# A graph network kernel: GpSimd's streams of gathers and scatters are paused in five different ways

## The reference, cut to what matters

```python
h = relu(layernorm(x)); x = x + gat(gat(h))          # attention over edges, 3 heads x 32, then 1 x 32
h = relu(layernorm(x)); x = x + rgcn(relu(rgcn(h)))  # per relation r: mean over its edges of h[src] @ W[r]
h = relu(layernorm(x)); x = x + f(h) + segment_sum(w * h[src] * h[dst] / (...), src)
h = relu(layernorm(x)); x = x + segment_sum((h[src] @ W_rel[type]) * e, dst)
```

## Time and profile before

| | us |
|---|---|
| median of 2 runs | 8182.64 (8157.38 to 8207.9) |
| the profiled execution | 8155.02 |
| its span | 8153.3 |
| GpSimd busy | 4271.4 (52%), 3949 instructions |
| VectorE busy | 3662.5 (45%) |
| TensorE busy with matmuls | 3196.6 (39%) |
| pass k, its 56 gathers | starts 1632.9 to 1705.5 |
| pass g1, its 336 gathers | starts 1752.0 to 2197.5 |
| pass g2, its 392 gathers | starts 2657.1 to 3258.0 |
| pass r1, its 392 gathers | starts 3537.0 to 4057.9 |
| pass r2, its 392 gathers | starts 4562.7 to 5158.4 |
| pass l2, its first gather | starts 5452.3 |
| pass l3, its gathers, then its scatters | starts 6955.2 to 7486.6, and 7488.1 to 8128.1 |

### The profile page before, as it was taken

The page is one execution under the profiler, slowest core; times in us unless marked ns, Lnnn a source line. Parts: engine busy times, 40 slices in busy tenths (PEclk is TensorE's granted clock), DMA queues, the critical chain, the costliest instruction groups (busy, mean ns, idle before and its releaser), DMA issues. The chain is left out here.

```text
span 8153.3 us, 45063 instructions
## 1 busy us (share of the span) xinstructions
PE 3196.6 (39%) x13056; PEld 2463.0 (30%) x13056; DVE 3662.5 (45%) x8866; ACT 1171.5 (14%) x1912; POOL 4271.4 (52%) x3949
## 2 busy tenths in 40 slices
PE   5799999830145104520077313541111100111232
PEld 3587755420134003410066212431111100111131
DVE  8533599741166216750034214784433217312464
ACT  0344445410023003300011000100000000000000
POOL 5544355557600665047700475118888880677565
PEclk9656799955566555555566555665555555555666
DMA  1111222201000212111022111122222223210011
GB/s 35 29 38 47 62 67 67 76 7 10 10 12 14 59 22 64 57 26 15 14 89 97 50 22 38 56 72 39 51 35 37 26 7 133 70 19 19 28 46 52
DMA packets 283355, 350.12 MB, mean 43 GB/s; under 512 B 133518, under 2 KB 204432, under 8 KB 281970
## 3 DMA queue, kind: packets, MB, share of 16 engines
q1 hardware_dynamic: 112158, 295.24, 10.8%
q0 software_dynamic: 169376, 41.40, 6.3%
q10 hardware_dynamic: 1576, 10.60, 0.5%
HBM read 231.06 MB, written 122.29 MB: 43 GB/s over the span
## 5 line engine op out<-in xcount | busy, mean ns | idle before, releaser
L2097 POOL DMA_INDIRECT r_ring<-t_rel,idx x392 | 385.7, 984 | 714.6 <-POOLq L122 503.7
L1456 POOL DMA_INDIRECT g_ring<-t_gat,idx x392 | 400.5, 1022 | 659.8 <-POOLq L122 458.4
L2320 POOL DMA_INDIRECT acc<-l_rows,l_uniq x392 | 629.9, 1607 | 121.1 <-issue 108.8
L507 POOL DMA_INDIRECT pay<-in_x,gidx x392 | 440.0, 1123 | 408.6 <-DVE a_act_t L592 288.4
L2307 POOL DMA_INDIRECT l_ring<-t_mix,idx x392 | 423.1, 1079 | 415.4 <-POOLq L122 293.0
L1786 POOL DMA_INDIRECT r_ring<-t_rel,idx x392 | 401.7, 1025 | 398.4 <-POOLq L122 278.1
L2582 PE MATMUL ps_l<-w_rel,l_pick 128*128 128x256 f32 x784 | 259.2, 503 | 844.5 <-DVE l_pick L2611 756.0
L2541 POOL DMA_INDIRECT l_ring<-t_last,idx x392 | 399.0, 1018 | 339.9 <-ACTq L2536 206.4
L2361 PE MATMUL ps_l<-l_msg,l_alike 128*128 128x16 f32 x784 | 176.1, 375 | 969.3 <-DVE l_msg L2424 897.6
L779 POOL DMA_INDIRECT t_sort<-pay,c_pos x392 | 386.1, 985 | 312.7 <-DVE c_pos L845 209.9
L871 PE MATMUL ps_c<-plane,c_hit 128*128 128x400 f32 x1568 | 544.2, 500 | 2.1 <-ACT c_hit L797 2.1
(11 more groups left out here) (528 smaller groups left out, 8211.6 us busy)
## 6 DMA issues: line engine op xcount, KB each, us to landing
c_rows_d<-row_dst SPq DMA_DIRECT2D x98, 256.0 KB
l_keys<-row_at SPq DMA_DIRECT2D x49, 512.0 KB
l_typs<-row_typ SPq DMA_DIRECT2D x49, 512.0 KB
g_hs<-t_gat SPq DMA_DIRECT2D x30, 660.0 KB
acc<-r_zero SPq DMA_DIRECT2D x60, 320.0 KB
t_rel<-r_row SPq DMA_DIRECT2D x30, 640.0 KB
r_hs<-t_rel SPq DMA_DIRECT2D x30, 640.0 KB
d_gain<-acc SPq DMA_DIRECT2D x30, 640.0 KB
```

Of the source, the lines that this page charges most:

```text
L507: pool.indirect_dma_start(pay[:, s, 8:PAY], None, x, bass.IndirectOffsetOnAxis(gidx[:, s:s + 1], 0)).then_inc(gat_in[s % LANES], 16)
L1456: pool.indirect_dma_start(ring[:, s % (NR * QN), :], None, t_gat2, bass.IndirectOffsetOnAxis(idx2[:, s:s + 1], 0)).then_inc(gat_in[s % LAN ...
L2097: pool.indirect_dma_start(ring[:, s % (NR * QN), :], None, t_rel2, bass.IndirectOffsetOnAxis(idx2[:, s:s + 1], 0)).then_inc(gat_in[s % LAN ...
L2320: pool.indirect_dma_start(acc[r], bass.IndirectOffsetOnAxis(uniq[:, s:s + 1], 0), rows[:, (s // ES) % RR, s % ES, :], None, compute_op=ALU.add
```

## The change

`behind(engine, landing, s, back)` is the old wait with a distance of its own: it waits for DMA s - back. `paced` stays as the case of 4. The passes then differ:

- k and g1, and the scatters of l3: at every column s that 8 divides, the wait is for the DMA just before (1 back), at the others for 4 back.
- g2: the wait stays at 4 back, and at every eighth column GpSimd writes one number per partition into a new tile `rest`.
- r1: a drain of GpSimd at every 16th column. The gathers of l3: a drain at every 32nd.
- r2: every gather waits for the one 2 before.

Passes a, c and l2 stay as they are.

```diff
+def behind(engine, landing, s, back, first=0):
+    n = s - back - first
+    if n >= 0:
+        engine.wait_ge(landing[n % LANES], 16 * (n // LANES + 1))
+
 def paced(engine, landing, s, first=0):
-    n = (s - first) // LANES
-    if n:
-        engine.wait_ge(landing[(s - first) % LANES], 16 * n)
+    behind(engine, landing, s, LANES, first)
@@ pass k, L953
-                        paced(pool, gat_in, s)
+                        behind(pool, gat_in, s, 1 if s % 8 == 0 else LANES)
@@ pass g1, L1116
-                        paced(pool, gat_in, s, EARLY)
+                        behind(pool, gat_in, s, 1 if s % 8 == 0 else LANES, EARLY)
@@ pass g2, L1455
+            rest = tmp("rest", [P, T // 8])
                         paced(pool, gat_in, s)
+                        if s % 8 == 0:
+                            nc.gpsimd.memset(rest[:, s // 8:s // 8 + 1], 0.0)
@@ pass r1, L1785
                             paced(pool, gat_in, s)
+                            if s % 16 == 15:
+                                pool.drain()
@@ pass r2, L2096
-                        paced(pool, gat_in, s)
+                        behind(pool, gat_in, s, 2)
@@ pass l3, gathers, L2540
                         paced(pool, gat_in, s)
+                        if s % 32 == 31:
+                            pool.drain()
@@ pass l3, scatters, L2550
-                        paced(pool, sent, s)
+                        behind(pool, sent, s, 1 if s % 8 == 0 else LANES)
```

## The result

The changed kernel took 7380.46 us (median of 2 runs, 7353.24 to 7407.68) against 8182.64: a ratio of 0.902, with a 95% interval of 0.883 to 0.921. The profiled execution took 7407.68 us with a span of 7406.0, 747.3 us less than the span before.

| us, from a pass's first gather to the next one's | before | after | difference | forecast |
|---|---|---|---|---|
| all up to g1's first gather | 1752.0 | 1754.9 | +2.9 | 0 |
| g1, one back at every eighth | 905.1 | 635.0 | -270.1 | -290 |
| g2, an own write at every eighth | 879.9 | 874.7 | -5.2 | +10 |
| r1, a drain at every 16th | 1025.7 | 649.1 | -376.6 | +6 |
| r2, two back | 889.6 | 804.8 | -84.8 | -300 |

A forecast was written before the change was run, and what follows sets the result against it. TensorE's late results beside GpSimd's DMA stream were taken as the bound. Terms k 0, g1 -290, g2 +10, r1 +6, r2 -300, l3 -20 + 3 on 8155.0 gave 7564, stated as 7570 us; 8-in-10 range 6950 to 8290.

The forecast's parts named there:

- What bounds the kernel: In k, g1, g2, r1, r2 and l3, TensorE's results come late while GpSimd streams; DMA rate or number in flight suspected.
- k and g1: One back at every eighth: k 0, its waits hidden; g1 freed at an average step of 1.50 us, -290 us.
- r2, -300: Pass r2: two back frees TensorE, with a step of 1.38 us per gather, worth -300 us.
- rival 1: Only one back frees; two back in r2 doesn't and costs +12 us; total 7876 us; chance 0.20.
- r1, +6: Pass r1: 24 drains at 0.25 us each cost 6 us and free nothing.
- the forecast's own criterion: Average step per DMA decides: 1.4 us is slow, 1.68 is not; g1's 1.50 between them counted as freed.
- rival 2: Any interruption frees, write and drain too: g2 -270, r1 -410, l3 some -60 more; 6808 us; chance 0.25, whole or part.
- g2, +10: Pass g2: the own write at every eighth column costs 10 us on the path and frees nothing.
- l3: Pass l3: scatters with one back -20 us, drains in the gathers +3 us; gathers not freed.
- Rival 3: No pause frees any pass; waits and writes only cost; 8268 us, no change by the measure; chance 0.16.
- The rule of the Trainium skill: DMA never contends with compute engines and TensorE never waits, so no GpSimd pause could help; set against the whole forecast.
- the fourth: No pause frees, every pause at its upper bound, drains and writes waiting 1.35 us in r1, g2, l3; 8390 us; chance 0.09.

The follow-up runs named there:

- e10: One back at every 16th column in g2 and l3's gathers, every eighth in r2; rest as in kernel before; stalling sitting, 7701.89 us against 8171.89.
- e7: One back at every 16th column in k, g1, g2, r1, r2 and l3, no other added pause; clean sitting, 6772.24 us against 6575.13 of kernel before.
- e11: Kernel before plus one back at every 16th in k, g1, every eighth in l3's scatters, a 128 x 256 write per r1 gather; stalling, 7717.67 us against 8171.89.
- e4: First run of one back at every 16th column in all these passes and l3's scatters; clean sitting, 6752.66 us beside 6558.43 of kernel before.
- e2: Kernel before plus a 128 x 256 write before every gather or l3 scatter, for an even step; clean sitting, 7053.75 us beside 6558.43.
- e1: A GpSimd drain at every 16th column in k, g1, g2, r1, r2 and l3, replacing all other pauses; clean sitting, 6887.19 us beside kernel before's 6558.43.
- e9: Drain at every 24th column in k, g1, every 32nd in r1; one back at every eighth in g2, r2, l3's gathers; clean, 6845.67 us against 6575.13.

## Why the prediction was right in its size, and where it was not

The sum gave 7564 and the profiled execution took 7408; the median, 7380, lies 190 us below the forecast 7570 and inside the range. Four of its six terms were within 20 us. That the total came so near is luck: r1 gave 383 us more than forecast and r2 215 less, and the two errors partly cancelled.

- **What bounds the kernel: right for such a sitting.** TensorE's results come late beside a fast stream, and freeing them was worth 270 us in g1 and 377 in r1. What I could not read from one execution is that this is not a property of the kernel: in a clean sitting it is gone. The rows of l3 in e10 and e7 show this at an equal step.
- **k and g1: right.** -270 against -290. The step came to 1.57 us (524.8 us over 335 steps), not 1.50, because the gathers lengthen from 1022 ns to 1087 once the other engines run; which of them does it is not shown.
- **r2, -300: the mis-sized term.** It gave -85. Two back was taken to free the pass, with a step of 1.38 us. It runs at about 1.30 to 1.32 and stalls, as rival 1 said. What ends the stall is a hold, for the ring is full:

```profile
4240.00:4297.00 57.00, 6.54 (x15) 3.93 (x15) 6.86 (x9) 2.02 (x4) 40.51 (x43) 0.50 0.09 13
4316.00:4500.00 184.00, 108.36 (x547) 90.72 (x547) 167.19 (x273) 24.86 (x60) 109.60 (x109) 0.75 0.26 74
```

```profile
4316.31 0.94 POOL L2107 DMA_INDIRECT r_ring<-t_rel,idx  x1 [19.31 <-PE r_ps L2138]
```

TensorE does 0.26 matmuls per us before the hold of 19.31 us and 2.97 after it. The kernel before has three holds in this pass, of 20.3 to 44.2 us, and falls back into the stall after the first two; the changed kernel does not. So two back does not free a stalled pass; whether it keeps a freed one free was not tried by itself. One back at every eighth frees the pass from its start and gave -243 in e10.
- **r1, +6: the step that failed.** "A drain has no row", and I took 0.25 us for it with 1.35 as the upper bound. It costs 2.43. That makes the step of r1 1.40 us by the waits alone, (15 x 1.25 + 3.67)/16, and 1.57 once the other engines run (612.3 us over 391 steps); it was freed, -377, near the -410 of rival 2. Reckoned as g1 was, from the 1.33 of the stream before, the right price gives 1.33 + 2.43/16 = 1.48, and the forecast's own criterion would have counted r1 among the freed, as it did g1 with 1.50. But the prediction took 1.25 as the base in r1 and g2 and 1.33 in g1.
- **g2, +10: right in kind.** The write costs nothing and frees nothing, -5.
- **l3: right in sum.** -16 against -17, and again by errors that cancel. The 12 drains cost 3.1 to 4.7 us each (idle of 3.41 to 5.01 us before the next gather), leave the step at 1.40 and free nothing: the gathers took 15 us more, for a forecast of 3. The scatters took 610 us for 640, for a forecast of 20 less.
- **Rivals.** Rival 2 ("any interruption frees") holds for r1 but not for g2 and l3's gathers; the even step of e11 shows that an interruption is not needed either. Rival 3 is what a clean sitting makes likely, with other prices: there the pauses of the other versions cost 194 (e4) to 495 us (e2) and give nothing. The changed kernel itself was not run in one.
- **The rule of the Trainium skill** that I set against the change, SBUF — State Buffer, "Who interferes with whom" (TensorE never waits on anyone), was read too widely: from it I took that no pause of GpSimd could give TensorE anything, and one back at every eighth took g1 from 0.54 matmuls per us to 2.33. Whether SBUF, which that section is about, has any part in the delay no run shows. The rule's price in the forecast is also muddled: no pause helping is rivals 3 and 4, 0.25 together, and the fourth alone has 0.09, not "a fifth".

What stays open: what makes a sitting stall, where TensorE's results are held, and whether the recording does it. Chips 12, 6 and 9 gave clean sittings, 12 and 15 stalling ones. There is no profile of the kernel before in a clean sitting, so that g1 and r1 are clean there without any pause is inferred from its 6575 us, which e7's kernel, with a pause at every 16th column, exceeds by 197.

## What to carry to other kernels

Read the time of the same kernel on several occasions before explaining it: here 24% lay between two kinds of sitting, with hardly any spread inside one, more than any edit gave. If a PE row ends long before its consumer starts while GpSimd streams indirect DMAs, find out first whether the stall is there in other sittings too, and without a recording if that can be had. Where it is real, one wait for the DMA just before at every eighth freed g1 and r2 from their start, for 1.39/8 = 0.17 us on a step of 1.25; an even step of 1.44 us freed r1. Where the stall is absent, the same is a loss. An average step read from a freed pass is no recipe, since it is in part a result of being freed. Price a drain in a stream of DMAs at 2.4 us and more.

## What the runs showed of the hardware that was not expected

- A drain of GpSimd behind a stream of indirect DMAs costs more the more DMAs lie between two drains, and the pass hardly matters. At every 16th the idle before the next gather has a median of 2.84 us in r1 and 2.71 in l3 (e1); at every 24th 3.08 in g1 (e9); at every 32nd 3.49 in l3 and 3.46 in r1 (e9). Without a drain it is 0.30. Waiting for the last DMA costs less, 1.39 us.
- A memset of 128 x 1 between two indirect DMAs is free (1.25 us a step with it and without), and one of 128 x 256 (0.33 us) adds 0.20, less than its own length.
- Even pass a, whose code is the same in all kernels and whose gathers are 2 us apart, ends earlier in clean sittings: its last gather starts at 844 to 882 us there and at 897 to 918 in stalling ones. The stretch from 500 to 700 us in e1 (clean) and in the kernel before:

```profile
500.00:700.00 200.00, 180.64 (x898) 157.31 (x896) 82.09 (x110) 94.72 (x175) 101.82 (x101) 0.70 0.19 56
```

```profile
500.00:700.00 200.00, 187.10 (x769) 161.32 (x767) 73.66 (x98) 82.32 (x151) 87.29 (x85) 0.57 0.16 46
```

TensorE does 898 matmuls at a granted clock of 0.70 against 769 at 0.57. Whether the lower clock is a cause or follows from the late results is open.
